# One program for attention, feed-forward and final phase: feed-forward's first steps merged into attention's last groups

## The reference

```python
x = x + tanh(g_xattn[0]) * mha(layernorm(x), ctx, ctx, W_Q, b_Q, W_K, b_K, W_V, b_V, W_O, b_O)   # 16 heads of 32
x = x + tanh(g_ffn[0])   * bitlinear_ffn(layernorm(x), w_gate, w_up, w_down)   # ternary weights, 8-bit activations, inner 2048
x = x + tanh(g_xattn[1]) * (softmax(layernorm(x) @ ctx.T) @ ctx)
x = x + tanh(g_ffn[1])   * mxfp4_linear(layernorm(x), weight, bias, delta_w, delta_act)
```

## Time and profile before

| | |
|---|---|
| median of 3 runs | 1613.41 us (1613.15 to 1620.27) |
| profiled execution | 1612.97 us |
| its span, first to last instruction | 1611.2 us |
| instructions | 24713 |
| mean granted TensorE clock | 0.953 of full speed |
| PE busy | 1478.4 us, 92% of the span |
| DVE busy | 1232.1 us, 76% |
| DMA engines' share | 57.4% |

### The profile page before, as it was taken

How to read it: one execution, slowest core, us unless ns; L and a number is a source line. 1 busy time by engine, 2 the same in 40 slices (tenths; PEclk the granted TensorE clock), 3 DMA queues, 4 the chain that set the end, 5 groups by cost and what they waited for, 6 DMA issues and landing times. The chain is left out here.

```text
span 1611.2 us, 24713 instructions
## 1 busy us (share of the span) xinstructions
PE 1478.4 (92%) x6994; PEld 937.4 (58%) x6994; DVE 1232.1 (76%) x2143; ACT 880.9 (55%) x1443; POOL 887.8 (55%) x1148
## 2 busy tenths in 40 slices
PE   5789999999999999989784999999999979999997
PEld 3466666566665566666432555555555447778785
DVE  4977677676778778787552888888888848999995
ACT  5156666665666565665442555555555535556552
POOL 3166766675775766765542443343334316777774
PEclk9799999999999999999777999999999989999997
DMA  6567858486694865857932444444444744556531
GB/s 203 157 214 193 250 150 254 166 223 183 164 285 140 227 226 153 273 144 221 250 66 62 102 109 108 110 108 111 114 111 108 192 133 134 158 181 197 162 87 56
DMA packets 234924, 261.13 MB, mean 162 GB/s; under 512 B 139836, under 2 KB 164936, under 8 KB 225096
## 3 DMA queue, kind: packets, MB, share of 16 engines
q1 hardware_dynamic: 234824, 259.95, 57.4%
HBM read 143.20 MB, written 78.68 MB: 138 GB/s over the span
## 5 line engine op out<-in xcount | busy, mean ns | idle before, releaser
L777 ACT ACTIVATE a_probs<-a_sc 128x512 f32<-128x512 f32 x512 | 300.7, 596 | 270.4 <-PE a_sc L642 268.4
L903 DVE TENSOR_REDUCE a_negmax<-a_mx 128x1 f32<-128x512 f32 x512 | 338.2, 674 | 89.2 <-PE a_mx L625 88.2
L998 POOL TENSOR_TENSOR a_acc<-a_acc,a_probs 128x512 f32<-128x512 f32 x248 | 311.1, 1285 | 6.1 <-ACT a_probs L777 5.0
L998 POOL TENSOR_TENSOR a_acc<-a_probs 128x512 f32<-128x512 f32 x124 | 157.0, 1285 | 239.5 <-ACT a_probs L777 238.7
L625 PE MATMUL a_mx<-a_stack 96*128 96x512 f32 x512 | 230.1, 449 | 34.4 <-DVE a_negmax L903 24.6
L1149 PE MATMUL bank<-wcode,b_xq 128*128 128x512 bf16 x1024 | 229.8, 383 | 10.5 <-DMA b_xq<-b_xcode 10.5
L642 PE MATMUL a_sc<-a_stack 97*128 97x512 f32 x512 | 215.4, 422 | 11.4 <-DMA a_stack<-a_mrow 9.8
L1149 PEld LDWEIGHTS bank<-wcode,b_xq 128*128 128x128 bf16 x1024 | 100.8, 99 | 134.7 <-DMA b_xq<-b_xcode 11.8
L914 DVE RECIPROCAL a_attn<-a_den 128x128 f32<-128x128 f32 x128 | 120.8, 947 | 72.6 <-PE a_den L680 58.4
L625 PEld LDWEIGHTS a_mx<-a_stack 96*128 96x128 f32 x512 | 102.2, 200 | 109.3 <-DVE a_negmax L903 59.9
L1187 ACT ACTIVATE b_sig<-bank,b_tok 128x512 f32<-128x512 f32 x128 | 87.5, 684 | 93.8 <-PE bank L1149 91.7
(11 more groups left out here) (171 smaller groups left out, 2652.1 us busy)
## 6 DMA issues: line engine op xcount, KB each, us to landing
a_stack<-spill SPq DMA_DIRECT2D x168, 256.0 KB, 7.2
spill<-k_part SPq DMA_DIRECT2D x56, 512.0 KB, 3.3
ctx_t<-k_wo SPq DMA_DIRECT2D x16, 1024.0 KB, 10.7
c_ct<-ctx_t SPq DMA_DIRECT2D x8, 2048.0 KB, 8.1
a_stage<-in_x_dram SPq DMA_DIRECT2D x32, 256.0 KB, 5.1
a_wsum<-in_L_ffn_w_gate_dram SPq DMA_DIRECT2D x8, 1024.0 KB, 6.3
attn_t<-a_attn SPq DMA_DIRECT2D x32, 256.0 KB, 4.5
a_wsum<-in_L_ffn_w_up_dram SPq DMA_DIRECT2D x8, 1024.0 KB, 6.6
```

Of the source, the lines that this page charges most:

```text
L777: nc.scalar.activation(probs[:, k, j, :], sc[i % 2][:], ACT.Exp, scale=SCALE).then_inc(exp_done, 1)
L903: nc.vector.tensor_reduce(negmax[:, g % 2, j, t:t + 1], mx[i % 2][:], axis=AX.X, op=ALU.max, negate=True).then_inc(mx_done, 1)
L998: nc.gpsimd.tensor_tensor(acc[:, j], probs[:, 0, j] if k == 1 else acc[:, j], probs[:, k, j], ALU.add)\
```

## The change

One program holds all three phases, in one Block. `attention_phase` becomes `attention_steps`, which returns its steps as the others do. `run_joined` becomes `run_chain`. Attention is emitted unrolled as before, and the first steps of feed-forward (its batches up to the start of its loop) are merged into it by time, feed-forward's tick 0 at attention's tick 5090 and 0.87 attention ticks for each of its own. Feed-forward and final phase keep their join.

```diff
+    merge(timed(ck1, late1, order1, range(begin1, end1), 0, 1, window1),
+          timed(ck2, late2, order2, range(begin2, lo2), origin2, scale2, window2))
+    if after_one:
+        after_one(engine)
     if hi2 > lo2:
         with engine.Fori(lo2, hi2) as it:
             emit(ck2, order2, window2, it)
...
-    JOIN, SCALE = 3165, 0.64
+    JOINS = ((5090, 0.87), (3165, 0.64))
...
-            clear_semaphores(nc)
```

```diff
+    xin = over("xin", [P, X4, D], F32, spot["xt"])
+    apart = over("apart", [P, 2, 2, C, P], F32R, spot["stage"])
+    x1 = over("x1", [P, X4, D], F32, spot["wsum"])
+    xq = over("xq", [P, 2, C, P], BF16, spot["stack"])
+    hid = over("hid", [P, 2, N], F32, spot["stack"] + 16384)
+    hq = over("hq", [P, 2, R, P], BF16, spot["stack"] + 40960)
...
+    banks = [mx[0], mx[1], work[1], sc[0], sc[1], den, work[0], pvb]
...
+    def den_free(engine):
+        engine.wait_ge(recip_done, G * T * NB)
...
+                if isinstance(it, int) and it + shift == 0 and t == 0:
+                    (att["mx_free"], att["sc_free"], att["sc_free"], att["den_free"])[m](pe)
+                    att["gu_codes"](pe)
```

The twelve code transposes are at other ticks, and the last group's closing steps come sooner (reciprocals, `norm_out`, `bias` and `store` of the last group of the last batch):

```diff
-            if g < T - 1:
-                for n, tick in enumerate((5, 35, 65, 100)):
-                    ck.add(base + tick, 9, "uturn", g, n)
+    for k, tick in enumerate((5, 35, 125, 150, 178, 206, 234, 290, 318, 346, 374, 402)):
+        ck.add(tick, 9, "uturn", k // CH, k % CH)
...
+            if g == G - 1:
+                ck.add(base + BURST + at["den"] + 4 + 2 * q, 7, "recip_last", g, q)
```

At the start, in the first batch only, the K projection of group 1 is emitted behind the first `max` (`qk_first`, `K_FIRST = 30` in place of 26), the first six quantise steps move from the projections to `max` 1 and 3 of group 0, the others come four `max` later, and POOL's split of W_V waits for W_K's:

```diff
+                if (g, side) == (1, K):
+                    ck.add(ahead(K_FIRST) + c, 3, "qk_first", g, side, c)
...
-                        slot_n = g * T * J + i - 1
+                slot_n = g * T * J + i - 5
+                if it + shift == 0 and slot_n == -4:
+                    dve.wait_ge(q_loaded, 16)
+                    for n in range(3):
+                        quantise(n)
+                if it + shift == 0 and slot_n == -2:
+                    dve.wait_ge(exp2_done, 2)
+                    dve.wait_ge(gated, 1)
+                    for n in range(3, 6):
+                        quantise(n)
...
+            pool.wait_ge(w_lo, SPLIT_AT[3])
```

More of the change, by code:

```diff
@@ L65, in run, with run_chain @@
             emit(it)
[L68 to L77, removed]
+def run_chain(engine, one, two, three, joins, after_one=None, after_two=None):
     def emit(ck, order, window, it):
@@ L87, in timed, with merge, plan @@
                 for it in its for shift, name, args in order if 0 <= it + shift < ck.batches]
[L89 to L103, removed]
+    def merge(*parts):
+        for _, window, it, shift, name, args in sorted((entry for part in parts for entry in part), key=lambda entry: entry[0]):
+            window(it, shift, name, args)
+    def plan(ck, late):
+        order = ck.order(late)
+        shifts = [shift for shift, _, _ in order]
+        lo = max(1, -min(shifts))
+        return order, -max(shifts), lo, max(lo, ck.batches - max(shifts)), ck.batches - min(shifts)
+    (ck1, window1, late1), (ck2, window2, late2), (ck3, window3, late3) = one, two, three
+    (origin2, scale2), (origin3, scale3) = joins
+    order1, begin1, _, _, end1 = plan(ck1, late1)
+    order2, begin2, lo2, hi2, end2 = plan(ck2, late2)
+    order3, begin3, lo3, hi3, end3 = plan(ck3, late3)
+    merge(timed(ck1, late1, order1, range(begin1, end1), 0, 1, window1),
+          timed(ck2, late2, order2, range(begin2, lo2), origin2, scale2, window2))
+    if after_one:
+        after_one(engine)
     if hi2 > lo2:
@@ L137, in sync_wait @@
     sp.sem_inc(held, 1)
[L140 to L149, removed]
 class Turns:
@@ L1001, in attention_phase, with sb, pb @@
[L1001 to L1004 removed]
+    def sb(name, shape, dt):
+        place[name] = here()
+        return ctx.enter_context(nc.sbuf_tensor("a_" + name, shape, dt))
+    def pb(name):
+        return ctx.enter_context(nc.psum_tensor("a_" + name, [P, 512], F32))
@@ new lines, in attention_steps @@
+    for g in range(G):
+        base = g * PERIOD
+        ck.add(base + BURST + 26, 9, "uload", g + 1, "sum")
+        ck.add(base + {1: 50, 2: -36}.get(g, 38), 9, "uload", g, "code")
+        ck.add(base + BURST + 2, 9, "sum", g, 0)
+        ck.add(base + BURST + 10, 9, "sum", g, 1)
+        ck.add(base + BURST + 2, 9, "uround", g, 0)
+        ck.add(base + BURST + 10, 9, "uround", g, 1)
+        ck.add(base + BURST + 12, 9, "uclip", g, 0)
+        ck.add(base + BURST + 20, 9, "uclip", g, 1)
+        ck.add(base + BURST + 29, 9, "ucode", g)
+        ck.add(base + BURST + 44, 9, "ustore", g)
@@ L1805, in _ @@
             def _(sp):
-                run_joined(sp, first["sync"](sp), then["sync"](sp), JOIN, SCALE, ffn["finish"])
+                run_chain(sp, one["sync"](sp), two["sync"](sp), three["sync"](sp), JOINS, att["finish"], ffn["finish"])
                 finish(sp)
```

1667 lines of the change are left out of this document (869 added, 798 removed).

## The result

The kernel after takes 1598.77 us in the median of four runs (1593.03 to 1599.51), the kernel before beside it 1613.49: a ratio of 0.989, 95% interval 0.987 to 0.992. It is faster, by 15 us between the medians where 33 were forecast, and lies above the forecast's range. The profiled execution took 1598.12 us with a span of 1596.3, 14.9 less than before.

What follows compares the result with a forecast made beforehand. PE was taken to bound the kernel nearly everywhere, so only its idle or slow stretches could be regained: 1612.97 - 9.5 + 3.0 + 2.5 - 24.1 - 4.5 = 1580.4, say 1580 us. Range 1568 to 1594 us.

Steps and rivals of the forecast that it cites:

- part 1: Last batch, group 1: new transpose ticks free SP's queue, the row of maxima lands in time; 9.5 us gained, bounds 7 to 9.8.
- part 4: Group 3 with two `o` projections merged in: 17.2 us from its first score to `gu` 0.
- part 5: Bank hand-over: `gu` 3 waits for reciprocals, second tile's `gu` 18.2 us after `gu` 0; 24.1 us gained from group 3's start.
- part 6: Kernel start: POOL's split waits for DVE's W_K split, quantise steps come later; 4.5 us gained, bounds 0 to 6.6.
- part 7: Everything else, such as counted-on semaphores, new addresses and banks, attention's earlier order and the loops: no change, 0 us.
- Part 2: Around groups 1 and 2: late row of maxima for group 2 and W_O's split across its scores cost 3 us, bounds 0 to 8.
- Part 3: Group 2: two feed-forward operations among POOL's additions lengthen the group by 2.5 us, bounds 1.3 to 4.
- The late first tile: Rival, merged stretch: a waiting feed-forward step stops both phases; price 10 to 20 us, 1592 to 1604, chance 0.13.
- The transposes: Rival, SP's queue: transposes delay groups 2 and 3's rows; 1608 us at 7.44 each; chance 0.05 including any unseen wait.

Runs made afterwards that it cites:

- kernel 3: Kernel after, with the last batch's second context store issued just behind group 1's row of maxima instead of ahead of it; 1593.61 us.
- kernel 7: On kernel 3: second code transpose also behind group 1's row of maxima, one more transpose moved from ahead of group 2's row to behind it; 1595.46 us.
- kernel 1: Kernel after with only its start edits taken back (third W_K projection, quantise steps and POOL's split in their old places); 1600.56 us.
- kernel 5: Kernel after with PSUM banks allocated in another order, so feed-forward and final phase use the physical banks of before; 1595.27 us.
- kernel 4: Kernel after with DVE's four last reciprocals in one piece, ahead of tile 1's quantise steps; 1595.28 us.
- kernel 9: Kernel after with the final phase's hardware loop written out; 1592.85 us, ratio 0.986.
- kernel 11: Kernel after with the edits of kernel 4, kernel 9 and kernel 10, tile 0's first steps earlier, and feed-forward's loop written out; 1587.16 us, ratio 0.984.
- kernel 12: On kernel 11: tile 0's loads issued still earlier, W_O's load moved behind group 2's row of maxima; 1588.77 us.
- kernel 10: On kernel 7: ACT's and DVE's split of W_O moved late into group 2; 1595.84 us.

## Why the prediction was wrong in size

By the table the forecast missed 17.7 us: 4.9 in part 1, 3.6 in part 4, 1.3 in part 5, 4.1 in part 6 (2.4 by the mean of all executions), 3.8 in part 7 and 3.4 in the middle of attention, less 3.4 that it charged too much for groups 1 and 2.

*Part 1, -4.6 for -9.5.* The step that failed is "with a store of the context still on its way I allow 5" us. `mrow` was issued right behind ACT's copy, as forecast, but landed after 10.1 us. The 2.3 us of the earlier trace rows came from a moment when SP's transposes had held the row back, and the same large transfers were issued well ahead of it: w_down's load 16.5 us and the store of the context 6.0 us. With the queue set free, 1 MB of w_down, 1 MB of context and 256 KB each for the bias, three fills and attention's store are issued within the 4.2 us ahead of 8 KB. Kernels 3 and 7 took pieces of that away: 8.0 and 5.0 us. Kernel 7 moved a transpose as well, so how much of its 3.0 us is the bytes' is not shown apart.

*Part 2, nothing for +3.* Neither of its two steps, the late row and the split across the scores, made group 1 longer. POOL's first addition comes 5.34 us after the first score and the twelve take 14.85 us, as before (5.35 and 14.83). The 1.1 us are PE's clock: after 2.40 us of idleness instead of 1.44 the denominator ran at a granted clock of 0.50 (before 1.00) and took 1.94 us instead of 1.07, and the first maximum behind it was as slow. In kernels 1 and 5, with the same order, group 1 takes 21.6 us as before. Group 2's row was issued 2.2 us after ACT's copy and landed 1.2 us ahead of the denominator. DVE's split of W_O ended at 809.73, 2.15 us after POOL's last addition, and so it did before (811.34, 2.16 us): what it costs at the start of group 2 was in the 22.0 us already. In kernel 7, with group 1 in time, W_O came too late, and group 2 took 26.8 us.

*Part 3, +2.4 for +2.5.* Right. The two operations stand where forecast, at 820.96 and 822.20, and POOL's additions with them take 17.26 us instead of 14.81. The table has only +1.0 in group 2 because the scores started late, after the slow denominator, so that the first addition came 4.7 us after the first score instead of 6.2; in kernels 1 and 5 it comes 5.9 and 6.2 us after it, and group 2 takes 24.3 and 24.6 us. Groups 1 and 2 together are 2.1 us longer than before here, and 2.1 to 3.3 in the five other kernels with the same order up to there.

*Part 4, 20.8 us for 17.2.* The failing steps are the clock and "less 1.5 because the matmuls of `o` fill gaps". Windows from group 3's first score to `gu` 0, after and kernel 3 (columns as in the earlier trace rows):

```profile
833.10:853.90 20.80, 19.28 (x92) 8.91 (x88) 8.57 (x17) 11.15 (x20) 6.40 (x13) 0.92 0.16 44
```

```profile
830.90:850.10 19.20, 17.70 (x92) 8.53 (x88) 8.57 (x17) 11.04 (x20) 6.42 (x13) 1.00 0.17 48
```

PE idles 1.5 us in both. At full clock the stretch takes 19.2 us, and the forecast's sum without the gaps was 18.7; the 1.6 us on top are a clock of 0.92 where I assumed 1.0, after a group 2 in which PE was as idle as before (busy for 18.5 of 23.0 us, before 18.9 of 22.0). In the other kernels the stretch takes 19.2 to 22.2 us; why the clock fell in one execution and not in another stays open.

*Part 5, 19.5 us for 18.2.* `gu` 3 starts 12.4 us after `gu` 0, exactly as worked out, for the reason given (kernel 4). What I left out is that PE, idle for 4.9 us, then runs at its lower level, 1.2 GHz (granted clock 0.52 from 866.3 to 869.2): pieces 3 of both halves take 1.86 and 1.58 us instead of 1.04 and 1.03.

*Part 6, 2.1 us for 4.5.* The relief of DVE is as in the earlier trace rows, and the rule on the shared ports named there fits once more: DVE's pieces 3.02 us with POOL held back, 7.21 in kernel 1. The failing step is the addition of two savings on one engine: DVE spends its 2 us waiting for the fills, and the deferred quantise steps make PE wait a little later, 3.17 us at 58.33 where before had 2.09.

*Part 7, +3.8 for nothing.* "Counting on from used semaphores changes values of waits, not waits" failed. Each start value of its own needs a register value of its own in the loop; kernel 9 gives 3.6 us in the tiles back (222.4 - 218.8). From tile 1's `gu` to the end its profiled execution takes 720.5 us, and those of kernels 11 and 12, without the loop too, 718.3 and 719.3 (after 722.9, before 719.1).

Of the rivals, none happened as a whole. The late first tile did not come: `gu` 0 came 20.8 us after group 3's first score with PE idle for 1.5 us of them. The transposes held SP for 2.5 to 7.2 us each, but SP issued group 2's row at 803.45, it landed 3.0 us later, and the denominator ahead of the scores came at 807.63, so that rival had no price.

## What to carry to other kernels

A landing time read behind a blocked queue does not hold once the block is gone; look up which large transfers will then be issued in the last microseconds ahead of the one that is waited for. A semaphore that counts on inside a hardware loop costs instructions between a wait and its work; where an engine has no slack in the loop, a short loop can be written out (measured in kernel 9). And a gain ahead of a step with a date of its own (here W_O's landing) is real only up to that date. And before a difference of 1 us in one profile is given a cause, the same stretch in other executions of the same order shows what it does by itself.

## What the runs showed of the hardware

- An 8 KB row of maxima landed 2.2 us after its issue (before, DMA share 0.79 around it), and 2.9, 3.0, 5.0, 7.9, 8.0 and 10.1 us in the kernels above (shares 0.96 to 1.08): the share says full or not, and does not say how late. What is issued just ahead counts: with W_O's 1 MB load 1.3 us ahead of it, group 2's row landed after 7.9 us in kernel 11 (6.2 and 6.0 in kernels 7 and 10), with the load behind it after 2.9 in kernel 12.
- In the loop with semaphores that count on, DVE started 0.37 us after PE's transposes began instead of 0.26, and ACT 0.71 instead of 0.63. That is below what any busy time shows; it made up to 0.19 us a tile and 3.1 us in the final phase.
- DVE's 128x2048 split took 2.29 us with POOL idle (kernel 7) and 4.84 us beside its additions (after, at 804.89), which stayed at 1.3 us each. Begun beside POOL's additions of group 1, it ended 2.14 to 2.16 us after POOL's last operation there in nine kernels, however early it began (3.5 to 6.1 us long): it waited until POOL stopped. In kernels 11 and 12, begun in the middle of group 2, it took 2.71 us, and the next addition 3.3 us instead of 1.3. The Trainium skill, page "SBUF — State Buffer", section "Who interferes with whom", has one of the two blocked, and the rows agree; which one pays was not the same in each run.
- The groups of attention in which PE falls to half clock differ between executions of the same instructions (mean clock 0.94 to 1.00 from 432 to 540 us); the stretch from 433 us to the last batch took 315.7 to 323.2 us with them.
